# Expert tiles of two halves, each with an expert of its own, in a fused block of linear attention and mixture of experts

## The reference

```python
mod = (_silu(c) @ wmod).reshape(16, 6, 1, -1)          # sa, ca, ga, sb, cb, gb
h = _layernorm(x) * (1 + ca) + sa
x = x + ga * attention(h)      # linear attention, 16 heads of 8, cumulative sums over the sequence
h = _layernorm(x) * (1 + cb) + sb
x = x + gb * ffn(h)

def ffn(s):                    # 4096 tokens
    h = rmsnorm(s @ W_in.T, in_norm_w)
    logits = h @ Wr.T                                   # 8 experts
    idx = top_k(logits + expert_bias, 2)
    gates = softmax of the 2 chosen logits, 0 elsewhere
    for e in range(8):
        gate = silu(h @ Wg[e].T); up = h @ Wu[e].T      # 128 -> 512
        oe = rmsnorm(gate * up @ Wd[e].T, enorm_w[e])   # 512 -> 128
        out = out + gates[:, e:e + 1] * oe
    return rmsnorm(out, out_norm_w) @ W_out.T
```

## Time and profile before

| | |
|---|---|
| Median of 3 runs | 454.98 us (454.23 to 456.43) |
| The profiled execution's own time | 456.44 us |
| Its span, first to last instruction | 454.6 us |
| TensorE busy (matmuls) | 364.9 us, 80% |
| VectorE, ScalarE, GpSimd busy | 337.4, 290.8, 250.6 us |
| Mean granted TensorE clock | 0.924 of 2.4 GHz |
| Expert stage, first to last gate matmul | 242.9 to 406.4 us |

### The profile page before, as it was taken

One profiled execution on the slowest core, in us unless ns is written; L12 is line 12 of the kernel. 1 busy time (PEld: TensorE's weight loads), 2 busy tenths in 40 slices (PEclk: granted clock), 3 DMA queues, 4 the chain that ended last, 5 costly groups with the idle time before them and its releaser, 6 DMA issues.

```text
span 454.6 us, 13206 instructions
## 1 busy us (share of the span) xinstructions
PE 364.9 (80%) x3903; PEld 319.2 (70%) x3904; DVE 337.4 (74%) x1113; ACT 290.8 (64%) x814; POOL 250.6 (55%) x221
## 2 busy tenths in 40 slices
PE   3379999869999999975107999999999999991474
PEld 2158877658888888864105998999999999980353
DVE  3328899657888888867386788789779888790585
ACT  2244687656777777734733778678778778772585
POOL 4359557557777788853630246456546546464331
PEclk9969999998999999997557999999999999996579
DMA  8895000000000000000142122222122222113923
GB/s 238 305 420 218 2 1 25 25 24 20 25 23 28 25 23 23 23 25 25 41 123 68 40 73 65 52 70 64 52 70 64 61 61 71 36 36 89 343 71 92
DMA packets 21907, 35.67 MB, mean 78 GB/s; under 512 B 3827, under 2 KB 17670, under 8 KB 21350
## 3 DMA queue, kind: packets, MB, share of 16 engines
q1 hardware_dynamic: 17206, 25.39, 18.0%
q0 software_dynamic: 4544, 9.39, 6.1%
q10 hardware_dynamic: 128, 0.53, 0.5%
HBM read 23.80 MB, written 13.47 MB: 82 GB/s over the span
## 4 chain that ended last, share of the span: by engine, by line
PE 47%; DVE 22%; issue 13%; DMA 6%; ACT 5%; POOL 4%; DVEq 1%; SPq 1%; another core or an unknown queue 1%; ACTq 0%; POOLq 0%
PE bank L1472 8%; PE bank L1473 7%; PE bank L1474 7%; DVE prod L866 6%; PE bank L1302 4%; PE bank L1489 4%; PE bank L1488 4%; PE bank L1487 4%; PE bank L1458 2%; PE bank L1376 2%; DVE st L829 2%; DVE wmaxs L969 1%; DVE rows L928 1%; DMA out<-prod 1%; DMA place_sb<-place 1%
## 5 line engine op out<-in xcount | busy, mean ns | idle before, releaser
L533 POOL DMA_INDIRECT expert_rows<-late,to_place x78 | 87.5, 1121 | 93.3 <-DVE late L1158 69.7
L499 POOL TENSOR_TENSOR kv<-kv,v 128x1024 f32<-128x1024 f32 x32 | 67.7, 2135 | 40.8 <-ACT kv L634 40.8
L1472 PE MATMUL bank<-late,w_hi 128*128 128x256 f16 x312 | 85.7, 275 | 1.4 <-issue 0.5
L520 POOL DMA_INDIRECT dispatched<-rows,pos x64 | 67.3, 1052 | 34.3 <-issue 17.7
L1473 PE MATMUL bank<-late,w_hi 128*128 128x256 f16 x312 | 85.6, 274 | 0.0
L1474 PE MATMUL bank<-late,w_lo 128*128 128x256 f16 x312 | 85.5, 274 | 0.0
L1302 PE MATMUL bank<-cst,kv 128*128 128x128 f32 x576 | 73.8, 283 | 3.4 <-POOL kv L499 2.5
L1147 DVE SCALAR_TENSOR_TENSOR kv<-bank,uscale,kv 128x512 f32<-128x512 f32 x78 | 58.2, 747 | 21.0 <-ACT kv L714 16.2
L1302 PEld LDWEIGHTS bank<-cst,kv 128*128 128x128 f32 x576 | 69.6, 198 | 4.9 <-POOL kv L499 3.2
L714 ACT ACTIVATE kv<-bank,descale 128x512 f32<-128x512 f32 x78 | 53.5, 685 | 28.3 <-PE bank L1474 27.2
L720 ACT ACTIVATE kv<-kv 128x512 f16<-128x512 f32 x78 | 49.0, 628 | 19.6 <-DVE kv L1147 16.9
(11 more groups left out here) (207 smaller groups left out, 790.0 us busy)
## 6 DMA issues: line engine op xcount, KB each, us to landing
late<-dispatched SPq DMA_DIRECT2D x39, 129.0 KB
late<-wguT SPq DMA_DIRECT2D x1, 4096.0 KB, 16.5
late<-expert_rows SPq DMA_DIRECT2D x1, 2064.0 KB, 12.9
gates_bc<-gate_rows SPq DMA_DIRECT2D x1, 2048.0 KB, 6.9
wd<-wdT SPq DMA_DIRECT2D x1, 2048.0 KB, 20.9
out<-prod SPq DMA_DIRECT2D x16, 128.0 KB, 1.8
expert_rows<-late,to_place POOLq DMA_INDIRECT x78
late<-expert_rows SPq DMA_DIRECT2D x2, 516.0 KB, 4.5
```

Source lines behind the costliest of these rows:

```text
L499: nc.gpsimd.tensor_tensor(kvt[:, 0:HD, :, :], k_in, v_in.to_broadcast([P, HD, H, HD]), ALU.mult).then_inc(kv_done[t], 1)
L520: pool.indirect_dma_start(hbuf, bass.IndirectOffsetOnAxis(ap=pos[:, p, t * K + k:t * K + k + 1], axis=0), rows[:, p, t, k, :], None).then_ ...
L533: pool.indirect_dma_start(ybuf, bass.IndirectOffsetOnAxis(ap=to_place[:, s, r:r + 1], axis=0), yt[:, s, r, :], None).then_inc(y_scat[s], 16)
L1472: mm(o, w_hi[:, w], hi, start=True, stop=False)
```

## The change

A tile still has 256 rows, but they are now two halves of 128 rows and each half has its own place in the table, with a row and an expert of its own. An expert's rows are filled up to a multiple of 128, not of 256. The table has 72 entries (`HALVES`) where it had 40, and there are 36 tiles (`TILES`) for 39: a first turn, a loop of seven turns, and a last turn, all of four tiles.

- SyncE loads each half by a transfer of its own.
- In gate and up each matmul of 256 columns becomes two of 128 columns, since the halves can have different weights. The weight's address is computed for each half.
- In the down projection the matmuls are as they were. The address is computed for each half where it was computed for both.
- VectorE weighs each half with its own row of `enorm`.
- The fillers, the regions' spare rows and the sizes of the buffers follow.

```diff
-TILES = (TOK * K + E * (R - 1)) // R
+TILES = -(-((TOK * K + E * (P - 1)) // P) // RB)
 TURNS = -(-TILES // TURN)
+HALVES = TURNS * TURN * RB
...
                 for s in range(tiles):
-                    row = sp.snap(row_regs[s], min_val=0, max_val=HROWS - R)
                     if again_turn(i):
                         sp.wait_ge(place_done, TURN * i + s - 3)
-                    sp.dma_start(slots[:, s], hbuf[bass.ds(row, R), :].rearrange("(p j) w -> p j w", j=RB)).then_inc(
-                        slot_ld[s], 16)
+                    for r in range(RB):
+                        row = sp.snap(row_regs[RB * s + r], min_val=0, max_val=HROWS - P)
+                        sp.dma_start(slots[:, s, r], hbuf[bass.ds(row, P), :]).then_inc(slot_ld[s], 16)
...
             def weigh(t, s, i, e):
                 dve.wait_ge(ysq_done, RB * (t + 1))
-                row = enorm[:, bass.ds(e * D, D)]
-                nc.vector.scalar_tensor_tensor(
-                    yt[:, s, :, 0:D], Y[s % 2][:, 0:RB * D].rearrange("p (r d) -> p r d", d=D), ydesc[:],
-                    row.unsqueeze(1).to_broadcast([P, RB, D]), ALU.mult, ALU.mult).then_inc(y_done[s], 1)
+                for r in range(RB):
+                    last = nc.vector.scalar_tensor_tensor(
+                        yt[:, s, r, 0:D], Y[s % 2][:, r * D:(r + 1) * D], ydesc[:], enorm[:, bass.ds(e[r] * D, D)],
+                        ALU.mult, ALU.mult)
+                last.then_inc(y_done[s], 1)
...
-            ex_regs = [pe.alloc_register(f"pe_expert{j}") for j in range(4)]
+            ex_regs = [pe.alloc_register(f"pe_expert{j}") for j in range(RB * TURN)]
...
                 for c in range(FC // 2):
-                    o = (G, U)[part][h][:, c * R:(c + 1) * R]
-                    w = bass.ds(e * F + (part * E * F + (h * (FC // 2) + c) * P), P)
-
-                    mm(o, w_hi[:, w], hi, start=True, stop=False)
-                    mm(o, w_hi[:, w], lo, start=False, stop=False)
-                    last = mm(o, w_lo[:, w], hi, start=False, stop=True)
+                    for r in range(RB):
+                        o = (G, U)[part][h][:, c * R + r * P:c * R + (r + 1) * P]
+                        hi, lo = (hT3[:, s % 2, n * R + r * P:n * R + (r + 1) * P] for n in range(2))
+                        w = bass.ds(e[r] * F + (part * E * F + (h * (FC // 2) + c) * P), P)
+
+                        mm(o, w_hi[:, w], hi, start=True, stop=False)
+                        mm(o, w_hi[:, w], lo, start=False, stop=False)
+                        last = mm(o, w_lo[:, w], hi, start=False, stop=True)
...
-                    w = bass.ds(e * (FC * D) + f * D, D)
                     for r in range(RB):
+                        w = bass.ds(e[r] * (FC * D) + f * D, D)
```

More of the change, by code:

```diff
@@ L84, in shape_constants @@
     place = (token * K + np.arange(K)).reshape(P, -1).astype(np.uint32)
-    filler = np.zeros(((E + SPARE) * R, HW), np.uint32)
-    filler[:, D] = TOK * K + np.arange((E + SPARE) * R)
+    filler = np.zeros(((E + SPARE) * P, HW), np.uint32)
+    filler[:, D] = TOK * K + np.arange((E + SPARE) * P)
     return c, place, filler
@@ L409, in _ @@
             for e in range(E // 2):
-                row = sp.snap(tail_regs[e], min_val=0, max_val=E * REGION - R)
-                sp.dma_start(hbuf[bass.ds(row, R), :], filler[e * R:(e + 1) * R, :]).then_inc(filled, 16)
+                row = sp.snap(tail_regs[e], min_val=0, max_val=E * REGION - P)
+                sp.dma_start(hbuf[bass.ds(row, P), :], filler[e * P:(e + 1) * P, :]).then_inc(filled, 16)
             sp.wait_ge(scattered[0], 16 * NT * K * (B // 2))
@@ L700, in _ @@
             for e in range(E // 2, E):
-                row = act.snap(tail_regs[e - E // 2], min_val=0, max_val=E * REGION - R)
-                act.dma_start(hbuf[bass.ds(row, R), :], filler[e * R:(e + 1) * R, :]).then_inc(filled, 16)
+                row = act.snap(tail_regs[e - E // 2], min_val=0, max_val=E * REGION - P)
+                act.dma_start(hbuf[bass.ds(row, P), :], filler[e * P:(e + 1) * P, :]).then_inc(filled, 16)
             act.wait_ge(gate_diff, 1)
@@ L1120, in _ @@
             dve.wait_ge(table_done, 1)
-            ex_regs = [dve.alloc_register(f"dve_expert{j}") for j in range(4)]
-            last_ex = [dve.alloc_register(f"dve_last_expert{n}") for n in range(2)]
+            ex_regs = [dve.alloc_register(f"dve_expert{j}") for j in range(RB * TURN)]
+            last_ex = [dve.alloc_register(f"dve_last_expert{n}") for n in range(2 * RB)]
             def experts(t):
-                dve.load(ex_regs, tile_expert[0:1, bass.ds(t, 4)])
+                dve.load(ex_regs, tile_expert[0:1, bass.ds(RB * t, RB * TURN)])
                 return [dve.snap(r, min_val=0, max_val=E - 1) for r in ex_regs]
@@ L1181, in turn_of_tiles @@
                         put_places(*later)
-                for n in range(2):
-                    dve.reg_mov(last_ex[n], ex[tiles - 2 + n])
+                for n in range(2 * RB):
+                    dve.reg_mov(last_ex[n], ex[RB * (tiles - 2) + n])
             put_hT(0, 0, 0)
@@ L1192, in _ @@
             for n in range(2):
-                weigh(TILES - 2 + n, LAST - 2 + n, TURNS - 1, dve.snap(last_ex[n], min_val=0, max_val=E - 1))
+                weigh(TILES - 2 + n, LAST - 2 + n, TURNS - 1,
+                      [dve.snap(last_ex[RB * n + r], min_val=0, max_val=E - 1) for r in range(RB)])
             def coefficients(g):
@@ L1493, in turn_of_tiles @@
             def turn_of_tiles(i, first=False, last=False):
-                ex, ahead = experts(TURN * i), None if first else pe.snap(last_ex, min_val=0, max_val=E - 1)
+                ex = experts(TURN * i)
+                ahead = None if first else [pe.snap(r, min_val=0, max_val=E - 1) for r in last_ex]
                 tiles = LAST if last else TURN
                 for s in range(tiles):
-                    t = TURN * i + s
-                    gate_up(t, s, i, ex[s], 0, 0)
-                    gate_up(t, s, i, ex[s], 0, 1)
-                    gate_up(t, s, i, ex[s], 1, 0)
-                    gate_up(t, s, i, ex[s], 1, 1)
+                    t, e = TURN * i + s, ex[RB * s:RB * (s + 1)]
+                    gate_up(t, s, i, e, 0, 0)
+                    gate_up(t, s, i, e, 0, 1)
+                    gate_up(t, s, i, e, 1, 0)
+                    gate_up(t, s, i, e, 1, 1)
                     if first and s == 1:
@@ L1504, in turn_of_tiles @@
                     if s:
-                        down(t - 1, s - 1, i, ex[s - 1])
+                        down(t - 1, s - 1, i, ex[RB * (s - 1):RB * s])
                     elif not first:
@@ L1511, in turn_of_tiles @@
                         transpose_rows(t + 2, s + 2 - TURN, i + 1)
-                pe.reg_mov(last_ex, ex[tiles - 1])
+                for r in range(RB):
+                    pe.reg_mov(last_ex[r], ex[RB * (tiles - 1) + r])
             pe.wait_ge(wlo_done, WN)
@@ L1521, in _ @@
             turn_of_tiles(TURNS - 1, last=True)
-            down(TILES - 1, LAST - 1, TURNS - 1, pe.snap(last_ex, min_val=0, max_val=E - 1))
+            down(TILES - 1, LAST - 1, TURNS - 1, [pe.snap(r, min_val=0, max_val=E - 1) for r in last_ex])
             def stage_d(b, p, n):
```

61 lines of the change are left out of this document (30 added, 31 removed).

## The result

The changed kernel takes 529.5 us (median of 4 runs, 526.2 to 529.8), the kernel before 455.7 beside it (454.2 to 459.0): a ratio of 1.159, 95% interval 1.152 to 1.165. Forecast were 534 us. The profiled execution took 526.21 us around a span of 524.4.

What follows compares the result with a forecast made beforehand. TensorE's array bounds the kernel now, its sequencer 93% occupied; doubled address instructions make the sequencer the bound. Expert phase +77.4, entry +1.1, last weighings +0.2 sum to +78.7 us: forecast 534 us, range 505 to 553.

Steps and rivals of the forecast that it cites:

- The step of the sequencer: TensorE's sequencer in gate, up and down: each register instruction takes about 0.12 us to the next, 0.113 to 0.133.
- the second rival: Sequencer's step shortens to 0.09 to 0.10 us in a drained queue: kernel 478 to 495 us, chance 0.07.
- The phase: Expert stage, first gate to last down instruction of the sequencer: 244.2 us for 166.8 before, +77.4.
- "rest" of a tile: Sequencer's time outside gate, up and down addresses: semaphore waits, transposes and L1483, 0.68 us a tile.
- the turn change: Sequencer between turns: 1.1 us each, eight make 8.8; loading eight registers for four counted as nothing, at most 2.4 more.
- Entry: Start of expert stage: four row transfers for two before TensorE starts, +1.1 us, covering the longer table operations too.
- the fillers: End of kernel: half as many filler rows written, 0, or a small gain if they were last to land.
- The four table operations: VectorE at stage entry: 576 elements for 320 add nothing to 1.6 us, beside the later transfer.
- VectorE's weighing: Expert stage: two operations of 128 elements at 0.344 us for one at 0.476, +0.21 us a tile, hidden.
- Hidden register work: Rival: sequencer's address work overlaps with handing on matmuls, array bounds, -8.7 us, 446 us; chance 0.04.
- Weight load as the bound: Rival: gate and up's weight loads, 0.098 us each, cannot hide under short matmuls: 519 us, or about 490; chance 0.05.
- The clock: Rival: TensorE, with array work 63% of the time, falls to 1.2 GHz: 595 us; chance 0.03.

Runs made afterwards that it cites:

- e2: Kernel before, 256-column matmuls kept, experts loaded twice and all addresses computed twice, 180 register instructions a turn for 115: 517.6 us, ratio 1.136.
- e8: Changed kernel with fused addresses computed before waits, next turn's experts loaded early, TensorE's loop written out: 441.2 us, ratio 0.983; 1.000 when repeated on another chip.
- e9: Kernel before with only TensorE's loop written out, turns one after the other: 447.7 us, ratio 0.997; the kernel before took 448.7 on that chip.
- e1: Changed kernel with address arithmetic fused, up to six register operations in one instruction, 88 a turn for 212: 461.6 us, ratio 1.011.

## Why the prediction was right

**The step of the sequencer.** It took 0.124 us from an instruction of L1476 to its L1478 and 0.113 back (medians of 576 and 540 pairs), the same medians as in the kernel before between L1472 and L1474. Gate and up took 3.91 us for 3.94 forecast, down 1.91 for 1.92. That a queue with nothing in it would shorten the step was the second rival: it does not. The rule that other instructions are read while a control instruction executes (the Trainium skill, Advanced Engine Details and Errata, Sequencer and Instruction Queues, Sequencer Loop) may hold for their reading, but it hides none of this: e2 adds register instructions alone and costs 14%.

**The phase.** 239.7 for 244.2 forecast. The mis-sized term is the "rest" of a tile, 0.68 us for semaphore waits and transposes. From down's last address to the next tile's first the sequencer took 0.64 us before (median), and the sum kept that; after it took 0.53: 36 x 0.11 = 4.0 too much. The two parts themselves give 36 x 0.04 = 1.4 less. Against these stands the turn change, where nothing was counted for eight registers instead of four: it takes 1.81 us in place of 0.53, 1.28 more and not 1.1, so 8 x 0.18 = 1.4 too little. The load alone lasts 0.25 longer, inside the bound of 0.3 that was given. Together -4.0, of -4.5.

**Entry.** +1.1 was forecast for the later transfers, with VectorE through beside them. It was nothing: from VectorE's copy of the totals to the first gate matmul both executions take 13.3 us (229.6 to 242.9, 226.7 to 240.1). SyncE loads no rows before its filler transfers have landed, and its wait for them (L416 before, L417 after) ended 9.1 us after the totals before and 7.0 after:

```profile
L416 SPq EVENT_SEMAPHORE  x1: 17/17/17, 238.7 to 238.7; - x1
```

```profile
L417 SPq EVENT_SEMAPHORE  x1: 17/17/17, 233.8 to 233.8; - x1
```

So the row transfers began 1.8 us sooner, which hides the 1.1. The prediction gave the fillers nothing, or a small gain if they were the last to land; they were, since SyncE's next wait, for the table and the scattered rows, passes within 0.15 us in both. That they land sooner because they are half as large fits, but no run tests it.

The four table operations did grow, to 0.74 us each,

```profile
L1096 DVE TENSOR_REDUCE texp<-prod x1: 741/741/741, 229.6 to 229.6; 1x72 f32<-1x576 f32 x1
```

and VectorE comes 1 us later to the copy of the first tile's transposes; before, it had idled there for just that long. So the bound changed hands at no cost. That the gate began at 240.0 and not at 244 is the first stage's variation, not the change.

**VectorE's weighing.** 0.343 us for each half, for 0.344 forecast, hidden as said:

```profile
L1159 DVE SCALAR_TENSOR_TENSOR late<-bank,ydesc,enorm x72: 341/343/351, 253.5 to 481.4; 128x128 f32<-128x128 f32 x72
```

**The rivals.** Hidden register work: no, starts are 0.24 apart by threes. Weight load as the bound: no, e8 runs gate and up at 0.056 us a matmul with register addresses, and 876 matmuls in 50 us are one in 0.057. The page TensorE: Matmul & The Clock Gate of the Trainium skill (Back-to-back issue gap) has about 81 ns for such a pair; these runs disagree with it. The clock: 1.00 in two of the three stretches and 0.97 in the first, where it stood at 0.50 from 292.5 to 295.9 after a turn change, although the array had work for about 65% of the time. But the evidence brought against this rival was weak. It set 63% of array work beside 65% of busy time in the last stage, which counts each matmul's latency; and in the changed kernel's last stage the clock does fall, with more busy time:

```profile
505.00:518.50 13.50, 10.11 (x53) 7.96 (x52) 11.69 (x47) 11.75 (x54) 5.03 (x8) 0.78 0.29 85
```

One argument for hidden register work was wrong as well. TensorE did wait for its sequencer before the change: 0.35 to 0.40 us from the last transpose to the next gate at seven of the turn changes, where 0.056 is the array's pace, and e9, without the loop, has a turn 0.3 us shorter. This is outside the forecast's sum, which goes by the sequencer's rows.

**The whole.** Forecast +78.7 on the profiled execution, measured +69.8, 8.9 less: 4.5 in the phase, 1.1 at the entry, 2.8 by the first stage's end, 0.1 at the tail, and 0.4 of rounding and between register rows and matmul rows. The three other runs of the median are 3.1 to 3.6 us above the profiled one, so the median, 529.5, came 4.5 below the forecast.

## What to carry to other kernels

An address from a register is an instruction on the engine that uses it. Count them against the matmuls they serve, part by part: at 0.12 us each, a pair takes 0.24 us, which three matmuls of 256 columns (0.33 us) hide and three of 128 (0.17 us) do not. Splitting a matmul by expert doubles the register instructions and leaves the array's time nearly as it was (2.62 and 2.69 us for gate and up). Before a weight address is given to each half of a tile, look at how full the sequencer is; it is not in the busy shares. And a TensorE that the profile shows 95% busy can still have work for only two thirds of the time (4.25 us of 6.6): read the starts of its matmuls, and the busy time of PEld.

## What the hardware showed unexpectedly

A register instruction's own 0.03 to 0.08 us says nothing of its cost: from one to the next are 0.113 us (one operation), 0.124 (up to three fused) and 0.132 (six fused, e1), so six operations in one instruction cost little more than one. A load of registers from memory takes 0.34 us for four and 0.59 for eight. The same program ran its expert phase in 157.7 us in one job and in 167.6 in another. The clock accounts for 1.5 us of that; the rest goes largely with gaps of up to 0.6 us, many inside groups of matmuls and once a turn, to which the profile gives no cause.
